# Weight loads and the clears of the seat rows, issued by ScalarE at the end of its slots instead of by SyncE

## The reference

```python
def _mxfp4_matmul(x, codes, scales, block_size=BLOCK):
    w = codes * jnp.repeat(scales, block_size, axis=0)
    return x @ w
...
q = _mxfp4_matmul(x, wq_codes, wq_scales) + bq      # k and v alike, each 2048 x 2048
scores = jnp.einsum('bqhd,bkhd->bhqk', q, k) / jnp.sqrt(jnp.float32(HEAD_DIM))
attn = jax.nn.softmax(scores, axis=-1)
out = jnp.einsum('bhqk,bkhd->bqhd', attn, v).reshape(B, S, NUM_HEADS * HEAD_DIM)
return _mxfp4_matmul(out, wo_codes, wo_scales) + bo
...
x = x + _layernorm(attention(_layernorm(x)))
x = x + _layernorm(experts(_layernorm(x)))          # silu(x @ Wg) * (x @ Wu) @ Wd, top 2 of 8
```

## Time and profile before

| | |
|---|---|
| Three runs | 2092.08, 2097.92, 2099.7 us |
| Span of the profiled execution (first to last instruction) | 2076.3 us |
| Median over that span | 21.6 us |
| PE busy | 1970.1 us (95%) |
| DVE busy | 1759.6 us (85%) |
| POOL busy | 1525.8 us (73%) |
| ACT busy | 1417.6 us (68%) |
| Mean granted TensorE clock | 0.974 |
| The 128 slots | about 45 to 1840 us of the span |

### The profile page before, as it was taken

One profiled execution on the slowest core, in us unless ns is written; L12 is line 12 of the kernel. 1 busy time (PEld: TensorE's weight loads), 2 busy tenths in 40 slices (PEclk: granted clock), 3 DMA queues, 4 the chain that ended last, 5 costly groups with the idle time before them and its releaser, 6 DMA issues.

```text
span 2076.3 us, 33234 instructions
## 1 busy us (share of the span) xinstructions
PE 1970.1 (95%) x10926; PEld 1700.0 (82%) x10926; DVE 1759.6 (85%) x2706; ACT 1417.6 (68%) x2686; POOL 1525.8 (73%) x1317
## 2 busy tenths in 40 slices
PE   7999999999999999999999999999999999985992
PEld 5888888888888888888888888888888888875882
DVE  6888889888889889988989888988999888977554
ACT  4776767677677667776777677776777667773454
POOL 2678778787778777886878777877888777976322
PEclk9999999999999999999999999999999999996996
DMA  4667666787678767776677667765677666771453
GB/s 97 158 160 181 163 162 160 162 184 162 156 165 179 171 147 174 169 165 158 149 161 173 143 153 154 173 158 139 163 166 173 147 139 147 190 177 51 133 151 104
DMA packets 238064, 322.66 MB, mean 155 GB/s; under 512 B 47686, under 2 KB 105798, under 8 KB 237894
## 3 DMA queue, kind: packets, MB, share of 16 engines
q1 hardware_dynamic: 234822, 312.15, 64.1%
q0 software_dynamic: 3072, 8.39, 1.4%
HBM read 35.68 MB, written 18.35 MB: 26 GB/s over the span
## 4 chain that ended last, share of the span: by engine, by line
PE 71%; SPq 11%; POOL 5%; DVE 5%; ACT 4%; DMA 2%; issue 2%; POOLq 0%; ACTq 0%; DVEq 0%
PE ps_a L749 17%; PE ps_s L621 12%; PE ps_s L622 11%; PE ps_s L623 11%; SPq L395 9%; PE ps_a L750 8%; POOL pT_both L518 4%; PE ps_a L621 3%; PE ps_a L622 3%; PE ps_a L623 3%; ACT probs L1038 2%; DMA pT<-probs 1%; DVE part_max L1393 1%; ACT pT_both L1055 1%; DVE probs L1418 1%
## 5 line engine op out<-in xcount | busy, mean ns | idle before, releaser
L518 POOL TENSOR_TENSOR pT_both<-pT,pT_both 128x512 fp32r<-128x512 f32 x1016 | 1289.5, 1298 | 346.4 <-ACT pT_both L1055 344.1
L749 PE MATMUL ps_a<-pT_both,v_both 128*128 128x512 f32 x2048 | 746.9, 398 | 0.5 <-POOL pT_both L518 0.5
L1038 ACT ACTIVATE probs<-ps_s,shift 128x1024 f32<-128x1024 f32 x512 | 566.7, 1110 | 259.2 <-DVE shift L1402 258.9
L1055 ACT ACTIVATE pT_both<-pT 128x512 fp32r<-128x512 f32 x1016 | 605.9, 630 | 194.5 <-DMA pT<-probs 161.3
L1418 DVE STREAM_TRANSPOSE probs<-probs 128x1024 f32<-128x1024 f32 x508 | 614.4, 1229 | 63.7 <-ACT probs L1038 62.7
L1393 DVE TENSOR_REDUCE part_max<-ps_s 128x1 f32<-128x1024 f32 x512 | 612.4, 1215 | 20.0 <-PE ps_s L623 18.5
L750 PE MATMUL ps_a<-pT_both,v_both 128*128 128x256 f32 x2048 | 575.6, 281 | 0.0
L749 PEld LDWEIGHTS ps_a<-pT_both,v_both 128*128 128x128 f32 x2048 | 387.1, 189 | 86.3 <-POOL pT_both L518 1.3
L621 PE MATMUL ps_s<-kT_hi,qT_hi 128*128 128x512 f32 x1024 | 407.3, 398 | 20.0 <-ACT probs L1038 16.8
L622 PE MATMUL ps_s<-kT_lo,qT_hi 128*128 128x512 f32 x1024 | 403.4, 394 | 0.0
L623 PE MATMUL ps_s<-kT_hi,qT_lo 128*128 128x512 f32 x1024 | 402.4, 393 | 0.0
(11 more groups left out here) (202 smaller groups left out, 2621.7 us busy)
## 6 DMA issues: line engine op xcount, KB each, us to landing
pT<-probs SPq DMA_DIRECT2D x2032, 128.0 KB, 2.3
x_rows<-zeros SPq DMA_DIRECT2D x46, 128.0 KB, 2.2
xg<-x_rows SPq DMA_DIRECT2D x46, 128.0 KB, 2.1
y_rows<-y_sb SPq DMA_DIRECT2D x46, 128.0 KB, 1.9
pT<-in_L_attn_x SPq DMA_DIRECT2D x4, 512.0 KB, 5.6
codes<-in_L_attn_wk_codes SPq DMA_DIRECT2D x16, 128.0 KB, 2.4
scales<-in_L_attn_wk_scales SPq DMA_DIRECT2D x64, 32.0 KB, 3.0
codes<-in_L_attn_wo_codes SPq DMA_DIRECT2D x16, 128.0 KB, 2.3
```

Source lines behind the costliest of these rows:

```text
L518: pool.tensor_tensor(pT_lo[:, p, :].rearrange("p (i n) -> p i n", i=Q4), pT[:, s % 2, g, :, t:t + 2, :].rearrange("p i t q -> p i (t q)"), ...
L749: nc.tensor.matmul(out_both, v_hi[:, h % 2, k, :], move, start=k == 0, stop=False)
L1038: nc.scalar.activation(out, src, ACT.Exp, bias=shift[:, s % SLOTS, r:r + 1], scale=SCALE, accum_out=sums[:, s % SLOTS, r, g:g + 1])\
L1055: nc.scalar.activation(pT_hi[:, p, :].rearrange("p (i n) -> p i n", i=Q4), pT[:, s % 2, g, :, t:t + 2, :].rearrange("p i t q -> p i (t q)" ...
```

## The change

`load` takes the issuing engine as an argument and moves out of SP's program. SP keeps the loads ahead of the slots, with the first `o` load among them now, and in the slots it issues `turn_blocks` alone. ACT issues the other 59 loads behind the last operation of its slots 0 (k), 2 (v), 4 (q) and 6 (o of the next head), and the 46 clears at the end of its slots 8 to 53. The semaphores that it waits for ahead of each load are those of POOL's `weights` of the load before. POOL's `weights` of `o` moves from slot 2 to slot 0 and that of `k` from slot 1 to slot 2. No computation changes.

```diff
         OUT = max(POST) + 1
 
 
+        src = {"k": (wk, sk), "v": (wv, sv), "q": (wq, sq)}
+
+        def load(eng, k, h, codes=codes, scales=scales):
+
+            if k == "o":
+                eng.dma_start(codes[:, :, :].rearrange("p c n -> p (c n)"),
+                             wo[bass.ds(h * P, P), :]).then_inc(w_loaded[k], 16)
+                for g in range(NG):
+                    eng.dma_start(scales[g * BLOCK:(g + 1) * BLOCK, :, :].rearrange("p c n -> p (c n)"),
+                                 so[bass.ds(h * NG + g, 1), :].to_broadcast([BLOCK, D]))\
+                        .then_inc(w_loaded[k], 16)
+            else:
...
         @block.sync
...
-            def load(k, h, codes=codes, scales=scales):
...
+            sp.wait_ge(w_ready["k"], 1)
+            load(sp, "o", 0)
             for n in range(HALVES):
                 h, s = divmod(n, NH)
-                more = h + 1 < H
-                if s == 0 and more:
-                    wait(sp, w_ready["q"], h + 1)
-                    if h == 0:
-                        sp.wait_ge(w_ready["k"], 1)
-                    load("k", h + 1)
-                if n == 0:
-                    wait(sp, w_ready["k"], 2)
-                    load("o", 0)
-                if s == 1 and h > 0 and more:
-                    wait(sp, w_ready["k"], h + 2)
-                    load("o", h)
-                if s == 2 and h == H - 2:
-                    wait(sp, w_ready["o"], h + 1)
-                    load("o", h + 1)
-                if s == 2 and h + 2 < H:
-                    wait(sp, w_ready["o"], h + 1)
-                    load("v", h + 2)
-                if s == 4 and more:
-                    wait(sp, w_ready["o"], h + 1 if h + 2 < H else H)
-                    if h + 2 < H:
-                        wait(sp, w_ready["v"], h + 3)
-                    load("q", h + 1)
                 if n != LAST:
                     turn_blocks(n)
...
-                if NH <= n < NH + NS:
-                    if n == NH:
-                        sp.wait_ge(sm["zeros_set"], 1)
-                    u, k = part_of(n - NH), n - NH - FIRST_SEAT[part_of(n - NH)]
-                    sp.dma_start(x_rows[u][k * P:(k + 1) * P, :], zeros[:, :]).then_inc(x_cleared, 16)
...
             for n in range(HALVES + 2):
                 h, s = divmod(n, NH)
-                if s == 1 and h + 1 < H:
+                if s == 0 and h < H - 1:
+                    weights("o", h)
+                if s == 2 and h + 1 < H:
                     weights("k", h + 1)
-                if s == 2 and h < H - 1:
-                    weights("o", h)
...
                 if s == NH - 1 and h + 1 < H:
                     k_hi(h + 1, 1)
+                if live(n) and s == 0 and h + 1 < H:
+                    wait(act, w_ready["o"], h + 1)
+                    load(act, "k", h + 1)
+                if live(n) and s == 2 and h + 2 < H:
+                    wait(act, w_ready["k"], h + 2)
+                    load(act, "v", h + 2)
+                if s == 2 and h + 2 == H:
+                    wait(act, w_ready["k"], h + 2)
+                    load(act, "o", h + 1)
+                if live(n) and s == 4 and h + 1 < H:
+                    if h + 2 < H:
+                        wait(act, w_ready["v"], h + 3)
+                    else:
+                        wait(act, w_ready["o"], h + 2)
+                    load(act, "q", h + 1)
+                if live(n) and s == 6 and h + 2 < H:
+                    wait(act, w_ready["q"], h + 2)
+                    load(act, "o", h + 1)
+                if NH <= n < NH + NS:
+                    if n == NH:
+                        act.wait_ge(sm["zeros_set"], 1)
+                    u, k = part_of(n - NH), n - NH - FIRST_SEAT[part_of(n - NH)]
+                    act.dma_start(x_rows[u][k * P:(k + 1) * P, :], zeros[:, :]).then_inc(x_cleared, 16)
```

More of the change, by code:

```diff
@@ L346, in sandwich_layer @@
         OUT = max(POST) + 1
+        src = {"k": (wk, sk), "v": (wv, sv), "q": (wq, sq)}
[8 more added lines that the diff above has]
+            else:
+                w, s = src[k]
+                eng.dma_start(codes[:, :, :],
+                             w.rearrange("(c p) f -> p c f", p=P)[:, :, bass.ds(h * DH, DH)])\
+                    .then_inc(w_loaded[k], 16)
+                for g in range(NG):
+                    row = s.rearrange("(c g) f -> g c f", g=NG)[g:g + 1, :, bass.ds(h * DH, DH)]
+                    eng.dma_start(scales[g * BLOCK:(g + 1) * BLOCK, :, :],
+                                 row.to_broadcast([BLOCK, DC, DH])).then_inc(w_loaded[k], 16)
         @block.sync
@@ L354, in _ @@
                 sp.dma_start(x_in[:, rows, :], xv[:, rows, :]).then_inc(x_loaded[g], 16)
-            src = {"k": (wk, sk), "v": (wv, sv), "q": (wq, sq)}
-            def load(k, h, codes=codes, scales=scales):
[L359 to L374, removed]
             sp.dma_start(wr_raw[:, :, :], wr.rearrange("(c p) e -> p c e", p=P)).then_inc(sm["wr_loaded"], 16)
[L377 to L380, removed]
+            load(sp, "k", 0)
+            load(sp, "q", 0, first_codes["q0"], first_scales["q0"])
+            load(sp, "v", 0, first_codes["v0"], first_scales["v0"])
+            load(sp, "v", 1, first_codes["v1"], first_scales["v1"])
             for dst, b in ((bias_all["q"], bq), (bias_all["k"], bk), (bias_all["v"], bv)):
```

## The result

| | median us | runs | lowest to highest |
|---|---|---|---|
| before | 2095.0 | 4 | 2091.41 to 2099.7 |
| after | 2114.58 | 4 | 2112.57 to 2115.75 |

After / before is 1.0092, 95% interval 1.0076 to 1.0108: 19.6 us slower, where 6 us faster was forecast. The time lies in the forecast's range, on the other side of no change.

What follows compares the result with a forecast made beforehand. The prediction took PE, busy 95% of the span, as the bound, with 17.4 us of waits in the slots to win. -17.4 + 11 gave -6 us, from 2097.9 to 2092 us, range 2080 to 2136.

Steps and rivals of the forecast that it cites:

- The old loss (term -17.4): PE's 17.4 us of waits in the slots, from loads between SP's turns and neighbouring POOL weights; nearly all should go.
- The new loss (term +11): ACT's issues between a turn's landing and the next exponential make PE late, adding 11 us over the heads.
- The loop over two slots: Landing, ACT's issues, ACT's next slot, POOL, SP's turn, landing: 25.05 us against PE's 25.2, before clears and turn variation.
- the forecast's slack of 1.1: ACT may be 1.1 us late before PE feels it, taken off once for each head's late loops.
- the rival: SP and ACT hinder each other's issues, 3.9 us for a load, 0.9 for a clear; 2102 to 2148 us, chance 0.32.
- the forecast case: ACT pays SP's 2.42 us for a load and 0.64 for a clear; 2092 us, chance 0.42.
- Free issues: Rival: ACT's issues are nearly free, under 1.2 us for a load, so no new loss; 2083 us, chance 0.23.
- Nothing moves: Rival: SP's turns start no earlier because POOL's low parts gate them; 2098 us, chance 0.03.
- The 0 to 5 us for transfers side by side: Loads running beside a turn in the slots instead of between two, priced at 0 to 5 us, taken as 0.
- near 11 us: Sign of being right: PE's waits in the slots move to slots 5 and 7 and come to near 11 us.

Runs made afterwards that it cites:

- e7: The changed kernel with loads and clears all issued by SP, each load ahead of the turn of its own slot; 2066.80 us, ratio 0.9970 to before.
- e2: The kernel before with only the 46 clears moved to the end of ACT's slots, all loads still on SP; 2086.24 us, ratio 0.9965 to before.
- e3: The changed kernel with loads and clears all issued by SP, each load behind the turn of its slot; 2175.98 us, ratio 1.0384 to before.
- e8: The changed kernel with ACT's loads and clears one operation earlier, ahead of the high part that waits for the turn's landing; 2066.64 us, ratio 0.9966 to before.
- e5: The changed kernel with clears back on SP and ACT's loads ahead of the high part that waits for the landing; 2085.11 us, ratio 0.9954 to before.
- e9: e7 with the clears moved to ACT, ahead of the high part that waits for the landing; 2087.25 us, ratio 0.9953 to before.

## Why the prediction was wrong

**The old loss (term -17.4): the mechanism was right, the size was not.** That loads between turns and neighbouring `weights` made it is borne out from two sides, by e7 (order alone) and e2 (0.6 us off SP, order unchanged). But "all but a few" of the 17.4 us was too much. The best kernels keep 7 to 10 us of slot loss (3 of it my yardstick's) and 7 to 11 us of PE's waits, and gain 7 to 10 us. Some 4 to 5 us are lost in head 14 in every kernel but e3 (8.0), and they were never the loads'. ACT's small operation `vb_hi`, done once for each head, shows what they come from; the row of after, with the same 6.0 us in before and in e8:

```profile
ACT vb_hi L1075 <- PE ps_a L598: 6.0, 1, 6.0
```

Head 14 does it for itself and, two slots on, for head 15 too, and this second one waits 6.0 us for PE's bias product of head 14, with the high parts and exponentials of slot 4 behind it. It is the only such wait of 16, and PE is late in slots 4 and 5. I have read this from the rows; no run takes it away.

**The new loss (term +11): here the forecast failed.** What the placing costs is after less e8, 26 to 29 us. The sum was -17.4 + 11 = -6; it should have read -7 + 27 = +20. The step that failed is the length of the loop over two slots and the count of the loops that pay for it. By heads, after lost more than e8 by 13.6 us in heads 1, 3 and 5 (forecast 6.6), by 5.9 in heads 2, 4 and 6 (3.3), by 2.4 in heads 7, 9, 11 and 13 (1), by 4.6 in heads 8, 10 and 12 (nothing) and by 0.9 in head 14. By its own steps:

1. *The loop over two slots* is the right mechanism, since e5 and e8 take the issues out of it and nothing else. PE's waits moved where the step said: after loses 11, 10 and 10 us at slots 3, 5 and 7, and 4 at slot 4, where before lost 17 at slot 4.
2. *Its length* was put at 25.05 us plus 0.64 for a clear plus 0.6 for turns: 26.3 with a clear, against PE's 25.2. In heads 1, 3 and 5 of after, the loops from slots 2 and 4 took 26.6 to 27.7, 27.1 on the mean, so they were late by 1.4 to 2.5 us instead of 1.1. Two terms were too small: load and clear and their gaps, from high part to high part, 3.2 to 3.7 us (mean 3.5) against 3.06, and turns of 11.2 us on the mean in these loops against 10.8. (In the same slots before has 11.4, so it isn't ACT's issues that make them long.) Two others were off and cancel: from the last high part to the start of the next turn 1.95 against 1.4, since POOL does the eight low parts back to back, 1.3 us each, and is itself 0.5 us behind ACT at the eighth; and ACT from its second high part to the last of the slot, 0.54 + 8.23 against 0.51 + 8.70. The landing (1.75 against 1.80) was right.
3. *The excess counts several times.* A loop that is late by 0.9 us more loses 0.9 us in each of three loops of an odd head. From the first exponential of slot 1 to that of slot 7, three loops, heads 1, 3 and 5 took 80.9, 82.7 and 81.3 us; less PE's 75.6 and the forecast's slack of 1.1 that gives 4.2, 6.0 and 4.6 us, and the heads lost 4.4, 6.1 and 4.7, against the forecast's 2.2. In the loops without clears of heads 9, 11 and 13, 25.3 to 25.9 us, it is late by 0.1 to 0.7, as forecast (0.45).
4. *Even heads were read too quickly.* Heads 2 and 4 lost 2.5 to 2.7 us each against 1.1, nearly all of it in one place, slot 2 to 3, where ACT does the value parts between the load and the exponential: 4.3 to 4.4 us from high part to high part, then 4.8 to the exponential. The sum used the loop of an odd head for both. That is also why heads 8, 10 and 12, with loads and no clears, lost 0.8, 1.0 and 3.1 us (2.0, 2.3 and 2.3 in the second profile) where the sum had nothing.

**The price of an issue.** The 2.42 us that the sum carried over from SP was one load. The 58 that SP issued behind its first turn in before took 2.61 us on the mean (median 2.48, 2.31 to 4.19), and no other engine of that kind was issuing. On ACT a load took 2.34 us in slots 0, and in slots 2, 4 and 6, beside SP's turn, 2.66 on the mean and up to 3.95. So ACT pays about what SP paid, and the forecast had taken a load shorter than the mean. The rows for the scales, of before and then of after (ns shortest, median, longest; first and last start):

```profile
L373 SPq DMA_DIRECT2D scales<-in_L_attn_wk_scales x64: 422/427/2104, 4.4 to 1624.8; - x64
```

```profile
L367 ACTq DMA_DIRECT2D scales<-in_L_attn_wk_scales x60: 448/449/491, 41.6 to 1641.1; - x60
L367 ACTq DMA_DIRECT2D scales<-in_L_attn_wq_scales x60: 448/506/1616, 100.8 to 1707.6; - x60
```

The load of k runs on ACT in slots 0, where SP isn't issuing, and all its 60 scales took 0.45 to 0.49 us; those of q run beside a turn, 0.51 in the median. Single issues of over 1 us are no sign of it, since SP had them up to 2.1 us when it issued alone. The clears, of after and of e2:

```profile
L1191 ACTq DMA_DIRECT2D x_rows<-zeros x46: 345/394/647, 157.3 to 808.4; - x46
```

```profile
L1193 ACTq DMA_DIRECT2D x_rows<-zeros x46: 326/327/376, 153.4 to 787.7; - x46
```

A clear on ACT that has no issue of ACT right ahead of it takes 0.35 us in after and 0.33 in e2, whether SP is issuing (7 and 17 times) or not (16 and 28 times). Right behind a load it takes 0.45 us while SP is still (2 times in after, and 0.49 on the mean of 17 in e8) and 0.57 on the mean beside a turn (21 times in after). So about half of the difference comes from what stands right ahead in the queue, and half from SP beside it. For a load SP's part is about 0.3 us, a fifth of what the rival had priced. It is seen on ACT's side only: a turn on SP took 10.72 us on the mean in after and 10.80 in before, and 10.69 in after where ACT issued beside it. The Trainium skill, Perfetto Trace Analysis, section "DMA Instruction — HWDGE (DVE, Sync)", tells of a descriptor generator under a lock that two sequencers share, but it names those of DVE and Sync, not ACT's. Somewhat longer issues beside the other engine would fit such a sharing; no run here shows the lock. And e5 and e8 show that the hindrance by itself is not what costs: at 2.86 us for a load e8 is faster than before. The rival said that it decides from 2.6 us upwards, 0.2 us above the forecast case. SP's own mean of 2.61 stood there already, so the sign was open with no hindrance at all, and what was wrong was to hold the forecast case for likelier.

**The other rivals.** Free issues are refuted by the rows above. "Nothing moves" is refuted by after's 98 us for the landing and by e2. The 0 to 5 us for transfers side by side were not seen: e5 and e8 have the same transfers beside each other and are faster than before. The Trainium skill, DMA: Bandwidth & Descriptors, section "Issuing engines are not separate DMA queues", says that issuing from another engine saves the sequencer's time alone, and that this is "usually small relative to the DMA itself". The runs agree: e7, with all issues on SP, is as fast as e8, with loads and clears on ACT (0.9970 and 0.9966). They add that some 2.7 us of a sequencer for each load, and up to 0.6 for each clear, are worth 1.3 to 1.4% when they stand in the wrong place.

**The signs.** Of the signs of being right most came: loads of about 2.4 us or a little more, POOL's waits for scales gone, 98 us for the landing, PE's waits moved to slots 3, 5 and 7. The one that failed is "near 11 us": PE's waits came to 28.4.

**What stays open.** Whether head 14's 4 us would go with its wait, why a turn of SP takes anything from 10.2 to 12.1 us, why the expert stage is 20 us longer on some chips, and whether e5 or e9 is really ahead of e2, e7 and e8.

## What to carry to other kernels

An issue on a compute engine is priced by its place more than by its length: put it ahead of an operation that waits anyway, not between the awaited landing and what hangs on it, unless the loop has room for it (e2's clears of 0.33 us had). Take the price of an issue from all the rows of its kind, not from one. Follow the loop through all its engines (landing, issue, compute, POOL, turn, landing) for each kind of slot, with the engines' own lateness, and if the sum comes within a few per cent of the bound, take it that it decides the sign. Before moving work to another engine, try the order alone: here it gave the same gain with no cost.

## What the runs showed of the hardware

- ACT's queue hands over an instruction as soon as its wait is met, and so runs ahead of the computing: in e8 the load begins at 201.12 beside the exponential of 200.94, though the exponential of 202.03, the copy of 203.11 and the high part of 203.38 stand ahead of it in the program. It passes no open wait: in after the load begins 0.01 us after the high part that waited for the landing, 209.78 to 209.79. So in the late loops here "behind the waiting operation" cost the full length of the issues, and "ahead of it" next to nothing.
- While issues hold the queue, the high part behind them is put down in the profile to PE's `ps_a`, which had long been free: 71.3 us in after, 22.2 in e8.
- The length of an issue hangs on what its own queue issued right before. The same clear takes 0.59 us on SP behind a turn (45 of 46 in before) and 0.35 after a pause (the other one), and on ACT 0.33 to 0.35 after a pause and 0.44 to 0.65 right behind the scales. The codes take 0.38 us on ACT; a scale row 0.43 on SP and 0.45 on ACT alone.
- The expert stage, same instructions, ran at a granted clock of 0.95 with 139 GB/s on one chip and at 0.88 with 114 GB/s on another.
